# Merging TensorE's two waits at the head of a node tile in a graph network's product stage

## What is computed

```python
deg_out = clip(segment_sum(1, src), 1); deg_in = clip(segment_sum(1, dst), 1)
for W, b, g, beta in layers:              # 8 layers
    agg = segment_sum((h * rsqrt(deg_out))[src], dst) * rsqrt(deg_in)
    y   = agg @ W + b                     # 512 x 512
    h   = gelu(layer_norm(y) * g + beta)
out = layer_norm(x + h)
```

## Time and profile before

| | us |
|---|---|
| median of 3 runs (lowest, highest) | 1611.01 (1607.53, 1611.39) |
| the profiled execution, its own time | 1612.99 |
| span of the profiled execution | 1610.7 |
| TensorE busy, as share of the span | 71% |
| mean granted clock of TensorE | 0.834 of full |

### The profile page before, as it was taken

The page is one execution under the profiler, slowest core; times in us unless marked ns, Lnnn a source line. Parts: engine busy times, 40 slices in busy tenths (PEclk is TensorE's granted clock), DMA queues, the critical chain, the costliest instruction groups (busy, mean ns, idle before and its releaser), DMA issues.

```text
span 1610.7 us, 30805 instructions
## 1 busy us (share of the span) xinstructions
PE 1140.8 (71%) x6235; PEld 865.5 (54%) x6235; DVE 915.6 (57%) x2206; ACT 491.4 (31%) x833; POOL 870.6 (54%) x1092
## 2 busy tenths in 40 slices
PE   7865386796796777976977896789778899950000
PEld 7643133765666656656656665766577676730000
DVE  6644676454463454544654564346543366658997
ACT  5332220433333223323323333333234333320110
POOL 1754201555456356455556465646567566658885
PEclk9655568898897898888989998999999999985555
DMA  0940001614416226135136225522266512249997
GB/s 12 363 166 2 2 1 41 182 59 151 130 72 197 71 97 203 53 130 158 59 126 190 77 78 180 172 77 76 99 199 189 150 72 78 78 152 357 392 395 290
DMA packets 98950, 224.52 MB, mean 139 GB/s; under 512 B 15408, under 2 KB 15408, under 8 KB 98880
## 3 DMA queue, kind: packets, MB, share of 16 engines
q0 software_dynamic: 34432, 104.72, 21.4%
q1 hardware_dynamic: 64448, 119.06, 20.2%
HBM read 137.91 MB, written 85.82 MB: 139 GB/s over the span
## 4 chain that ended last, share of the span: by engine, by line
PE 54%; POOL 13%; issue 10%; DMA 10%; DVE 6%; ACT 3%; ACTq 2%; DVEq 1%; POOLq 1%; SPq 0%
PE ps_y L1256 12%; PE ps_y L1257 10%; PE ps_y L1261 10%; PE ps_a L1236 8%; DMA rows<-h_rows,slot 7%; POOL agg_t L518 5%; POOL rows L460 5%; PE ps_y L1252 4%; POOL agg_t L525 3%; PE ps_a L1151 2%; DVE agg_t L640 2%; ACT agg_t L1005 2%; PE ps_a L1217 1%; DMA w_raw<-in_bs 1%; PE ps_y L1170 1%
## 5 line engine op out<-in xcount | busy, mean ns | idle before, releaser
L1236 PE MATMUL ps_a<-sel,rows 128*128 128x128 f32 x2560 | 368.4, 301 | 182.7 <-DMA rows<-h_rows,slot 120.3
L1236 PEld LDWEIGHTS ps_a<-sel,rows 128*128 128x128 f32 x2560 | 337.6, 211 | 215.1 <-issue 212.3
L468 POOL TENSOR_TENSOR s_lo<-agg_t,s_hi 128x512 fp32r<-128x512 f32 x168 | 217.3, 1295 | 297.0 <-ACT s_hi L1047 297.0
L460 POOL DMA_INDIRECT rows<-h_rows,slot x290 | 278.8, 961 | 152.1 <-issue 111.7
L1042 ACT ACTIVATE agg_t<-ps_a 128x508 f32 x320 | 190.7, 596 | 388.3 <-PE ps_a L1236 367.6
L1256 PE MATMUL ps_y<-w_hi,s_hi 128*128 128x512 f32 x672 | 288.3, 429 | 10.1 <-ACT s_hi L1047 10.1
L815 DVE TENSOR_SCALAR sel<-iota,by_tile 128x128 f32<-128x128 f32 x344 | 123.8, 364 | 285.9 <-PE ps_a L1236 208.5
L1257 PE MATMUL ps_y<-w_lo,s_hi 128*128 128x512 f32 x672 | 270.5, 403 | 0.0
L888 DVE BATCH_NORM_STATS2 small<-ps_y 128x6 f32<-128x512 f32 x168 | 117.4, 699 | 172.1 <-PE ps_y L1261 171.0
L1261 PE MATMUL ps_y<-w_hi,s_lo 128*128 128x512 f32 x672 | 184.5, 397 | 0.0
L1256 PEld LDWEIGHTS ps_y<-w_hi,s_hi 128*128 128x128 f32 x672 | 129.6, 193 | 75.3 <-issue 52.5
(11 more groups left out here) (204 smaller groups left out, 1311.8 us busy)
## 6 DMA issues: line engine op xcount, KB each, us to landing
h_rows<-rows SPq DMA_DIRECT2D x168, 256.0 KB, 2.0
h_rows<-agg_t SPq DMA_DIRECT2D x1, 20480.0 KB, 59.2
agg_t<-in_x SPq DMA_DIRECT2D x78, 256.0 KB, 5.8
out<-agg_t SPq DMA_DIRECT2D x78, 256.0 KB, 5.4
w_raw<-in_Ws SPq DMA_DIRECT2D x32, 256.0 KB, 3.0
rows<-h_rows,slot POOLq DMA_INDIRECT x290, 3.7
rows<-in_ln_g SPq DMA_DIRECT2D x8, 256.0 KB, 3.7
rows<-in_ln_b SPq DMA_DIRECT2D x8, 256.0 KB, 4.5
```

The costliest lines, as they stand in the source:

```text
L460: g.indirect_dma_start(out=rows[:, k, :], out_offset=None, in_=table[:, :], in_offset=bass.IndirectOffsetOnAxis(ap=slot[:, k:k + 1], axis=0))\
L468: g.tensor_tensor(s_lo[:, k, :, :], agg_t[:, :, bass.ds(c * P, P)], s_hi[:, k, :, :].bitcast(f32), ALU.subtract).then_inc(lo_ok, 1)
L1236: m = mm(ps_a[k % GS][:, b, :], rows[:, k, b * P:(b + 1) * P], sel[:, k % GS, :], start=True, stop=True)
```

## The change

TensorE no longer waits on `t_ok`; its wait on `hi_ok` stands ahead of the bias product in place of it. So that `ps_y[k]` is still free when the bias product starts, `high(j)` on ScalarE waits on `t_ok` of tile j-2 where it waited on `y_ok` of tile j-2. On GpSimd `inverse(j)` stands ahead of `low(j+2)` in the loop.

```diff
@@ w_stage of GpSimd
                     for k in range(2):
+                        inverse(base + c + k, k)
                         low(base + c + k + 2, c + k + 2, k)
-                        inverse(base + c + k, k)
@@ high of ScalarE
             def high(j, c, k):
-                hold(y_ok, done(j - 1))
+                hold(t_ok, done(j - 1))
@@ w_stage of TensorE
                         j = base + c
-                        pe.wait_ge(t_ok, done(j + k - 1))
+                        pe.wait_ge(hi_ok, done(j + k + 1))
                         pe.sem_inc(pe_tick, 1)
                         mm(ps_y[k][:, :], ones2[:, :], b_rows[:, :], start=True, stop=False)
-                        pe.wait_ge(hi_ok, done(j + k + 1))
-                        pe.sem_inc(pe_tick, 1)
                         for b in range(KB):
```

## The result

| | us |
|---|---|
| before, median of 5 runs (lowest, highest) | 1611.01 (1607.53, 1611.83) |
| changed, median of 5 runs | 1617.31 (1614.96, 1619.69) |
| ratio, 95% interval | 1.0047 (1.0032 to 1.0062) |
| profiled execution of the changed kernel, own time; span | 1614.96; 1613.1 |

The change makes the kernel slower by 0.5%: 7.5 us by the ratio, with an interval of 5.1 to 10; the two medians are 6.3 us apart. The execution that was profiled is the fastest of the five; its span is 2.4 us above that of before.

A forecast was written before the change was run, and what follows sets the result against it. TensorE was taken to set the pace in the product stage. Steady tiles, ScalarE and GpSimd at 0 and first tiles at +4.2 us, on the median of 1611.0, gave 1615.2 us, range 1598 to 1621.

The forecast's parts named there:

- The gaps belong to the operand's rows: TensorE's steady tiles: both gaps around the 2-row bias come from the shape change and stay; removing the wait brings 0.
- B: Rival, steady tiles: the wait made the gap behind the bias, which closes, saving 33.6 us, to 1581.6; chance 0.11.
- C: Rival, bias's border: part of the gap is queue time, 0.08 us per wait with count, saving 14 us, 1601.2; chance 0.08.
- The Trainium skill's rule: TensorE at the bias product's borders: changing tiling mode drains the array first, so both gaps stay and the edit brings 0.
- 50 to 100 ns for reading a semaphore: Counter-evidence, TensorE's queue: at this cost in line, 168 waits less would be worth 8 to 17 us.
- The new wait hidden by 0.3 us: Steady tiles: the chain from last product through centring and high half reaches TensorE 0.3 us before the next-but-one bias load.
- ScalarE and GpSimd at 0: Steady tiles: the later high half, the earlier inverse and the later low half move nothing on the path; 0 us.
- the late high without the swap: GpSimd in its old order: the inverse would end at 1300.3, about when its scaling starts (1300.25).
- The first tiles, +4.2 us: Each stage's first tile: the bias, now behind the wait for the first high, is laid bare; 4.2 us lost in all.
- the lower bound of 3.2: First tiles' loss in all, us, if the clock rises at the same moment as before, returning part of the delay.
- the middle of the two bounds: First tiles: 4.2 us, taken between 5.2 at most and 3.2 in all.
- Same against slower: Whole kernel: verdict drawn at 0.3% or 4.8 us; same 0.47, slower 0.32, faster 0.21.

The follow-up runs named there:

- wide_before: Kernel before with the bias operands filled up with zeros from 2 to 128 rows, both TensorE waits left: 1706.68 us, ratio 0.9637.
- rows64: Kernel before with bias operands of which the product takes 64 rows, both waits left: 1764.21 us in one run, against 1770.97 before.
- rows96: Kernel before with bias operands of which the product takes 96 rows, both waits left: 1706.23 us in one run, against 1770.97 before.
- more_waits: Kernel before with four satisfied waits and counts behind the bias product instead of one: 1614.70 us against 1609.27, ratio 1.0032.
- wide_after: Changed kernel with the bias operands filled up with zeros from 2 to 128 rows: 1728.56 us, ratio 0.9755 to the kernel before.
- swap_only: Kernel before with only GpSimd's inverse moved ahead of the low half: 1759.76 us, ratio 1.0000 to the kernel before.
- merge_only: Changed kernel with GpSimd's old order, low half ahead of the inverse: 1764.07 us, ratio 1.0019 to the kernel before.
- first_ahead: Changed kernel with the bias product of each stage's first tile again ahead of the wait for the high half: 1759.19 us, ratio 0.9999 to before.

## Why the prediction was right

- **The gaps belong to the operand's rows.** Right, and now shown: `wide_before` closes both with all waits in place, `rows64` keeps them, `rows96` has none. Rivals B and C, which priced the wait at 0.20 and 0.08 us, have no place in the steady tile (`more_waits`). Of C's price something is true elsewhere: on an idle array a wait with its count cost 0.15. The range, 1598 to 1621, would have taken C's time as well, so it is the unchanged gaps of 0.24 and 0.35 us and not the time that bear the forecast out.
- **The Trainium skill's rule** (TensorEngine Tiling (Array Packing), Key Properties: a change of tiling mode drains TensorE) fits: 0.20 us at each border, and none elsewhere. No row shows the drain itself. That 64 rows make the gap and 96 do not fits the page's list of configurations, which has 128, 64 and 32 rows. The Trainium skill's 50 to 100 ns for reading a semaphore (Advanced Engine Details and Errata, Network/Comms) were not to be seen in a steady tile; on the idle array a wait together with its count took 0.15 us.
- **The new wait hidden by 0.3 us.** Right: 0.5 us between the high's end and the bias load, less some 0.14 for TensorE's start, is nearly 0.4. The latency from centring to high was 0.20 to 0.21, not 0.27. `wide_after` shows the same chain at work as soon as a tile is 0.4 us shorter.
- **ScalarE and GpSimd at 0.** Right, by `swap_only` and by the time lines. For the late high without the swap the prediction had the inverse end at 1300.3, about when its scaling starts (1300.25). `merge_only` shows the inverse 0.06 us ahead of that scaling: the reckoning was right to 0.1 us, but fell on the wrong side of the edge. VectorE is not held even without the swap; what the swap buys is room, 3.1 us of it, and no time.
- **The first tiles, +4.2 us.** The mechanism is shown by `first_ahead`; the size was too small. The traces of before and after alone give 5.0 us by the first products and 3.4 at the fourth tile, as if part came back; over six traces it is 5.5 and 5.9, and nothing comes back. So the lower bound of 3.2, which had the clock rise at the same moment as before, has no support, and the middle of the two bounds was not the place to be. The sixth and the eighth stage were priced at full clock, 0.43 us; in the changed kernel's trace their bias runs at half clock, and their first products are 0.69 and 0.74 us late. The timed runs gave +7.5 (5.1 to 10) and, on another chip, +3.5 (1.2 to 5.8); 5.9 lies in the first interval and just above the second. The steady tiles are equal in all these traces.
- **Same against slower.** The likeliest of the three was "same", drawn at 0.3% or 4.8 us. By that line the time came out as "slower" (0.47%, the interval from 0.32%), and inside the range: 1617.3 against a forecast of 1615.2. The term that was too small is that of the first tiles, by 1 to 2 us by the traces and by 3 if the first session is taken as it stands.

## What to carry to other kernels

An idle time that stands beside a wait need not be the wait's. Ask what else the two instructions differ in, and look for a place where the same wait stands without the gap; here one row (the load of the low half) was enough. Here a product with 2 or 64 rows between full ones cost 0.20 us at each of its two borders, and filling its operand up with zeros took both away (64 us of 1771). And before two waits are merged into the later one, look at what ran between them in the first turn of the loop, and at how much room the other engines' round trip has once a gap elsewhere is closed.

## What was new about the hardware

- A product of 64 or 2 rows between products of 128 rows: two gaps, and a tile of thirteen products takes 3.35 or 3.37 us; with 96 or 128 rows 2.97 and 2.95.
- Four satisfied waits with counts in TensorE's queue behind a running product: 0 us; on an idle array 0.15 each.
- After 2.3 us without work three overwritten products did not bring full clock back: the granted clock was 0.50 under them in six heads of eight, and seven first tiles began at half clock. Eight such products right behind the last gather product kept it full in all eight.
